# Graph attention in float32, one core: loads by graph in every step, a third buffer for transposed blocks, the reciprocal moved, the first graph reordered

## What is computed

```python
q, k, v = proj(Wq, bq), proj(Wk, bk), proj(Wv, bv)          # [32, 8, 256, 32]
scores = einsum('bhqd,bhkd->bhqk', q, k) * 32 ** -0.5
scores = scores * (adj + adj)[:, None]                      # a mask with values, not of zeros alone
attn = softmax(scores, axis=-1)
ctx = einsum('bhqk,bhkd->bhqd', attn, v)                    # heads put side by side: [32, 256, 256]
out = layernorm(x + einsum('bse,fe->bsf', ctx, Wo) + bo)    # [32, 256, 256]
```

## Time and profile before

| | |
|---|---|
| device time, 3 runs | median 437.6 us (437.01 to 439.08) |
| the profiled execution | 432.45 us, its span 430.8 us |
| PE busy | 383.4 us, 89% of the span |
| DVE busy | 387.9 us, 90% |
| ACT busy | 360.5 us, 84% |
| POOL busy | 249.6 us, 58% |
| DMA | mean 214 GB/s; 248 `carried<-boxes` of 192.0 KB, 124 `v_boxed<-v` of 64.0 KB, 16 masks and 16 x of 512.0 KB, 15 `xt` of 512.0 KB |

### The profile page before, as it was taken

How to read it: one execution, slowest core, us unless ns; L and a number is a source line. 1 busy time by engine, 2 the same in 40 slices (tenths; PEclk the granted TensorE clock), 3 DMA queues, 4 the chain that set the end, 5 groups by cost and what they waited for, 6 DMA issues and landing times.

```text
span 430.8 us, 12136 instructions
## 1 busy us (share of the span) xinstructions
PE 383.4 (89%) x3628; PEld 291.0 (68%) x3628; DVE 387.9 (90%) x1592; ACT 360.5 (84%) x1223; POOL 249.6 (58%) x379
## 2 busy tenths in 40 slices
PE   8968999998989899998999999899898999997682
PEld 6755767776767676675777667677766767775452
DVE  4687999999999999999899999989999999999965
ACT  4588899888888888888988888899888789988760
POOL 3330656748385664748567474856747385554455
PEclk9999999999999999999999999999999999999998
DMA  8548869788887978878797888889788787978632
GB/s 288 168 107 217 235 165 304 175 265 217 232 242 181 303 159 252 247 202 263 192 295 182 243 242 210 254 203 294 178 251 228 163 256 178 276 170 214 155 90 73
DMA packets 58658, 92.28 MB, mean 214 GB/s; under 512 B 7777, under 2 KB 47970, under 8 KB 58594
## 3 DMA queue, kind: packets, MB, share of 16 engines
q1 hardware_dynamic: 45266, 66.35, 60.8%
q10 hardware_dynamic: 13328, 25.17, 16.9%
HBM read 26.22 MB, written 8.39 MB: 80 GB/s over the span
## 4 chain that ended last, share of the span: by engine, by line
ACT 31%; PE 20%; DVE 16%; SPq 12%; issue 11%; DMA 7%; POOL 1%; ACTq 0%; DVEq 0%; POOLq 0%
ACT probs L705 24%; SPq L202 8%; DVE probs L502 8%; PE ctx_bank L396 5%; DMA v_boxed<-v 5%; DVE boxes L520 5%; PE proj_bank L325 4%; PE out_bank L343 4%; SPq L211 4%; PE row_bank L256 3%; ACT turned_probs L713 3%; ACT inverse L719 2%; PE turn_bank L273 1%; ACT kq L733 1%; DVE top L502 1%
## 5 line engine op out<-in xcount | busy, mean ns | idle before, releaser
L705 ACT ACTIVATE probs<-probs,low_top 128x256 f32<-128x256 f32 x512 | 254.7, 504 | 41.5 <-DVE low_top L511 40.4
L502 DVE CUSTOM_DVE_ANT_0 probs<-row_bank,adj_rows 128x256 f32<-128x256 f32 x512 | 188.0, 416 | 5.1 <-PE row_bank L256 4.8
L520 DVE STREAM_TRANSPOSE boxes<-probs 128x1536 f32<-128x1536 f32 x62 | 109.7, 1769 | 1.0 <-DMA carried<-boxes 1.0
L705 ACT ACTIVATION_READ_ACCUMULATOR probs<-probs,low_top 128x1 f32 x512 | 99.3, 194 | 0.0
L325 PE MATMUL proj_bank<-xt_parts,w_parts 128*128 128x512 f32 x360 | 99.3, 411 | 0.0
L325 PEld LDWEIGHTS proj_bank<-xt_parts,w_parts 128*128 128x128 f32 x360 | 63.0, 188 | 30.2 <-issue 19.6
L256 PE MATMUL row_bank<-kq 32*128 32x256 f32 x1024 | 73.3, 400 | 5.2 <-DVE top L502 3.9
L396 PE MATMUL ctx_bank<-carried,v_boxed 128*32 128x256 f32 x744 | 59.5, 382 | 19.1 <-DMA v_boxed<-v 16.1
L842 POOL COPY wide<-shares 128x512 f32<-128x512 f32 x32 | 19.5, 610 | 74.9 <-DVE shares L528 74.9
L396 PEld LDWEIGHTS ctx_bank<-carried,v_boxed 128*32 128x32 f32 x744 | 31.2, 109 | 43.5 <-issue 30.7
L413 PE MATMUL out_bank<-w_parts,ctx_parts 128*128 128x256 f32 x372 | 51.5, 287 | 9.9 <-issue 6.7
(11 more groups left out here) (85 smaller groups left out, 467.2 us busy)
## 6 DMA issues: line engine op xcount, KB each, us to landing
carried<-boxes SPq DMA_DIRECT2D x248, 192.0 KB, 4.0
adj_rows<-in_adj ACTq DMA_DIRECT2D x16, 512.0 KB, 6.6
xr<-in_x ACTq DMA_DIRECT2D x16, 512.0 KB, 6.9
v_boxed<-v SPq DMA_DIRECT2D x124, 64.0 KB, 2.5
out<-result ACTq DMA_DIRECT2D x31, 256.0 KB, 4.8
xt<-in_x_t SPq DMA_DIRECT2D x15, 512.0 KB, 4.2
xt<-in_x_t SPq DMA_DIRECT2D x2, 256.0 KB, 3.2
w_whole<-in_wk ACTq DMA_DIRECT2D x2, 128.0 KB, 3.4
```

The lines of the kernel that those rows point to most:

```text
L502: last = nc.vector.tensor_tensor_reduce(probs[:, h % RING, t * S:(t + 1) * S], row_bank[j][:, t * S:(t + 1) * S], adj_rows[:, (g // 2) % 2 ...
L520: nc.vector.transpose(boxes[:, n % 2].rearrange("p a h (f q) -> p (h f) a q", q=D), probs[:, first:first + BOXED, :].rearrange("p h (f a k ...
L705: last = nc.scalar.activation(tile, tile, ACT.Exp, bias=low_top[:, g % 2, J * c + j, t:t + 1], accum_out=sums[:, g % 2, t, j * T + c:j * T ...
```

## The change

- `xt`, masks and x are loaded by graph (for `xt`: by half of the feature rows) instead of by pair: 256 KB in every step. Masks of graph g + 2 are issued behind ACT's third head, x of graph g behind its seventh, one `xt` half in every step of SP. Each half has a semaphore.
- `boxes` has three buffers instead of two.
- `divide(g - 1)` goes from the end of DVE's step g - 1 into step g, behind the second head's row maxima.
- The first graph has an order of its own on PE, DVE and ACT: the second pair's keys are projected ahead of the first values, `rows(1)` follows at once, and the bias is made in step 1.

The diff, without the lines around it:

```diff
+BOXES = 3
...
-        boxes = sb("boxes", [P, 2, J, BOXED, P])
+        boxes = sb("boxes", [P, BOXES, J, BOXED, P])
...
-        xt_in, x_in, adj_in, stored, carried_in, v_in = (
-            [sem(f"{name}{n}") for n in range(2)] for name in ("xt_in", "x_in", "adj_in", "stored", "carried_in", "v_in"))
+        stored, v_in = ([sem(f"{name}{n}") for n in range(2)] for name in ("stored", "v_in"))
+        x_in, adj_in, carried_in = ([sem(f"{name}{n}") for n in range(4)] for name in ("x_in", "adj_in", "carried_in"))
+        xt_in = [[sem(f"xt_in{n}_{t}") for t in range(T)] for n in range(2)]
...
-            def load_x_t(pair):
+            def load_x_t(pair, t):
...
-                    sp.wait_ge(first_low, T)
-                wait(sp, xt_low, T * (pair - 2))
-                sp.dma_start(xt[:, pair % 2].rearrange("p t s -> p (t s)"), x_t[pair]).then_inc(xt_in[pair % 2], 16)
+                    sp.wait_ge(first_low, t + 1)
+                if pair > 2:
+                    sp.wait_ge(xt_low, T * (pair - 3) + t + 1)
+                sp.dma_start(xt[:, pair % 2, t, :], x_t[pair][:, t * 2 * S:(t + 1) * 2 * S]).then_inc(xt_in[pair % 2][t], 16)
...
-                                 boxes[D * i:D * (i + 1), n % 2].rearrange("p j h f -> p j (h f)")
-                                 ).then_inc(carried_in[n % 2], 16)
+                                 boxes[D * i:D * (i + 1), n % BOXES].rearrange("p j h f -> p j (h f)")
+                                 ).then_inc(carried_in[n % 4], 16)
...
-            load_x_t(1)
+            for t in range(T):
+                load_x_t(1, t)
...
-            load_x_t(2)
-            load_x_t(3)
+            for pair in (2, 3):
+                for t in range(T):
+                    load_x_t(pair, t)
...
-                if g % 2 == 1 and is_pair(g // 2 + 4):
-                    load_x_t(g // 2 + 4)
+                if g > 0 and is_pair((g + 1) // 2 + 3):
+                    load_x_t((g + 1) // 2 + 3, (g + 1) % 2)
...
-                    for c in range(T):
-                        pe.wait_ge(carried_in[c], 64 * (g + 1))
+                    for n in range(T * g, T * g + T):
+                        pe.wait_ge(carried_in[n % 4], 64 * (n // 4 + 1))
...
+            for half_ in range(2):
+                project_kq(1, 0, half_)
...
-            make_bias()
+            rows(1)
+            for half_ in range(2):
+                project_kq(1, 1, half_)
+            project_v(1)
+            turn_probs(0)
...
+                if g == 0:
+                    return
...
-                if 0 < g < B:
+                if g < B:
...
+                if g == 1:
+                    make_bias()
...
-                if h % (4 * J) == 0 and h % (2 * H) == 0:
-                    dve.wait_ge(adj_in[(g // 2) % 2], (g // 4) * 16 + 16)
+                if h % H == 0:
+                    dve.wait_ge(adj_in[g % 4], (g // 4) * 16 + 16)
...
-                wait(dve, carried_in[n % 2], 64 * (n // 2))
+                if n >= BOXES:
+                    dve.wait_ge(carried_in[(n - BOXES) % 4], 64 * ((n - BOXES) // 4 + 1))
...
-                nc.vector.transpose(boxes[:, n % 2].rearrange("p a h (f q) -> p (h f) a q", q=D),
+                nc.vector.transpose(boxes[:, n % BOXES].rearrange("p a h (f q) -> p (h f) a q", q=D),
...
+            read_first_q(0)
...
-            for c in range(T):
-                read_first_q(c)
+            read_first_q(1)
...
+                    if j == 1 and n % T == 0 and n > 0:
+                        divide(n // T - 1)
...
+                if g == 1:
...
-                if 0 <= g < LAST:
-                    divide(g)
...
-            def load_masks(pair):
+            def load_masks(g):
...
-                wait(act, rows_used, 16 * (pair - 1))
-                act.dma_start(flat(adj_rows[:, pair % 2]), adj[pair]).then_inc(adj_in[pair % 2], 16)
-            def load_x(pair):
-                wait(act, y_ready, 2 * (pair - 1))
-                act.dma_start(flat(xr[:, pair % 2]), x[pair]).then_inc(x_in[pair % 2], 16)
+                wait(act, rows_used, H * (g - 3))
+                act.dma_start(adj_rows[:, (g // 2) % 2, g % 2].rearrange("p t s -> p (t s)"),
+                              adj[g // 2][:, (g % 2) * T * S:(g % 2 + 1) * T * S]).then_inc(adj_in[g % 4], 16)
+            def load_x(g):
+                wait(act, y_ready, g - 3)
+                act.dma_start(xr[:, (g // 2) % 2, g % 2].rearrange("p t e -> p (t e)"),
+                              x[g // 2][:, (g % 2) * T * E:(g % 2 + 1) * T * E]).then_inc(x_in[g % 4], 16)
...
+            load_masks(1)
...
-                        copy_v(0)
...
-                    if s == 1 and g % 2 == 0 and is_pair(ahead):
-                        load_masks(ahead)
+                    if s == 1 and g == 0:
+                        copy_v(0)
+                    if s == 2 and is_graph(g + 2):
+                        load_masks(g + 2)
...
-                    if s == 2 and g % 2 == 0 and is_graph(g):
-                        load_x(g // 2)
-                    if s == 3 and is_graph(g + 1):
+                    if s == 6 and is_graph(g):
+                        load_x(g)
+                    if s == (3 if g > 0 else 5) and is_graph(g + 1):
...
-                    if s == 3 and is_pair(ahead):
+                    if s == (3 if g > 0 else 4) and is_pair(ahead):
...
+                pool.wait_ge(xt_in[pair % 2][t], 16 * loads(pair))
...
-                    pool.wait_ge(xt_in[pair % 2], 16 * loads(pair))
...
-                if b == 0:
-                    if pair == 0:
-                        pool.wait_ge(bias_ready, 1)
-                    pool.wait_ge(x_in[pair % 2], (pair // 2) * 16 + 16)
+                if pair == 0 and b == 0:
+                    pool.wait_ge(bias_ready, 1)
+                pool.wait_ge(x_in[2 * (pair % 2) + b], (pair // 2) * 16 + 16)
```

2 lines of the change are left out of this document (1 added, 1 removed).

## The result

The changed kernel takes **417.25 us** (median of 6 runs, 414.61 to 418.86) against 436.89 us before (median of 6 runs, 435.11 to 439.08): a ratio of 0.9547 with a 95% interval of 0.9506 to 0.9589, 4.5% less time. Its profiled execution is one of these runs, with 418.86 us and a span of 416.3 us. Throughout, a median is of all runs of a kernel, while a ratio leaves out those over 1.5% above the kernel's fastest.

What follows compares the result with a forecast made beforehand. Bound by the ring of reciprocals and first maxima and by late blocks at weigh_v in alternate steps; 432.45 - 16.9 (27 steps) - 5.5 (first graph) = 410.05 profiled, with the 5.15 us distance 415.0 us, range 409.5 to 424.

Steps and rivals of the forecast that it cites:

- The ring of the reciprocals: Once per graph DVE's reciprocals wait for ACT's last exponential (20.1 us), ACT's next first exponential for DVE's maxima (40.4 us).
- T = (17.33 + d) / 2: Lower limit on step T from the loop through PE's weigh_v; d is transpose end to last block landing.
- the 11.92 forecast: Mean step in us forecast for 27 steps, instead of 12.547, a gain of 16.9 us.
- DVE's floor, 11.82: A dense DVE step without its 0.41 us wait: 11.82 us, below which no step was to go.
- d = 6.5: Forecast us from transpose end to last block landing with loads by graph, no longer alternating between 6.0 and 7.3.
- the bound of 7.3: Upper bound in us for the new transpose-to-landing time, seen in one late delivery; the lower was 6.0.
- The first graph, 5.5 us: New order at the start: graph 3 to start at 47.2 us instead of 52.68, a gain of 5.5 us.
- The end, nothing: Step 30 is already 11.76 us and nothing behind it is changed, so no gain at the end.
- Three buffers, at most 1 us: Third block buffer removes DVE's wait before box, 1.0 us in all; at most 1 us, contained in the 11.92.
- 5.15 us between profiled execution and median: Median of three runs before lay 5.15 us above the profiled execution (437.6 against 432.45); same distance assumed after.
- 410.05 forecast for the profiled execution: Sum of the gains: 432.45 - 16.9 - 5.5 = 410.05 us, span 408.4.
- The rival by the constant part of a transfer: Slower, 3%: constant part occupies the queues, 2.2 us for each of 47 added transfers, step 13.7, about 463 us.

Runs made afterwards that it cites:

- the kernel that does not depend on them: Changed kernel with weigh_v(g - 2) behind project_v(g + 1) on PE and scale_context(g - 2) behind box(2g - 1) on DVE: 426.4 us, ratio 0.971.

## Why the prediction was right, and where it was not

The median of 417.25 us lies 2.25 above the 415.0 forecast and inside the range. The steps, in the order in which the prediction made them:

- **The ring of the reciprocals**: right. The wait went from 20.1 to 1.9 us; undoing the move alone costs 3.1 points. That it opens the way to steps shorter than 12.20 was shown by the kernel with the move undone, whose shortest common step is 12.22.
- **T = (17.33 + d) / 2**: the form right, the constant 0.2 too large. The loop runs over two steps, so its own test is their sum: from 205.32 us, where VectorE begins graph 16, to 229.25 it is 23.93 us, with a d of 6.79 for the blocks of graph 15, which PE needs in the second of these steps: d + 17.14. In 12 of the 14 places where PE waited over 0.3 us for blocks at the full clock the sum is d + 17.14 to within 0.02, and the same constant is the common one in the kernels with loads by pair. With the median d of 6.63 T is then 11.89. Without the two bad steps the mean is (327.39 - 16.19 - 13.49) / 25 = 11.91, against the 11.92 forecast. The steps do not settle at T but go 11.65, 12.0 and more, because a late `weigh_v` is made up for in the next step.
- **DVE's floor, 11.82**: 11.65 measured, though 11.76 stood in the earlier trace rows. The stretch of the earlier trace rows has no gap but the 0.41 us that I took off. About 0.08 of the 0.17 goes with that wait: in a dense step the operation behind `add_residual` starts 0.61 us after it, ahead of its end, and in the stretch its whole 0.69 us passed first. The rest is hundredths, over some fifty operations.
- **d = 6.5**: 6.6 in the common step. Left out were single landings of 9.1 and 8.5 us; the bound of 7.3 was that of one row, and the kernel before had no longer one than 8.0 in its profile. The steps behind them took 16.19 us (fourth stretch above) and, by ScalarE's timeline, 13.49, so they cost (16.19 - 11.92) + (13.49 - 11.92) = 5.8 us, of which 1.6 is the lower clock in the first (last section).
- **The first graph, 5.5 us**: graph 3 starts 52.68 - 48.16 = 4.5 us earlier, and I gave the gain to the wrong edit. The order has 1.4 us of it (1.9, counted from the first exponential); the reciprocals alone bring 2.2 (2.7). The rows at the start:

```profile
11.12 1.15 PE L264 MATMUL row_bank<-kq 32*128 32x256 f32 x16
...
17.03 0.42 DVE L521 CUSTOM_DVE_ANT_0 probs<-row_bank,adj_rows 128x256 f32<-128x256 f32 x1 [0.56 <-PE row_bank L264]
...
14.28 0.51 ACT L728 ACTIVATE probs<-probs,low_top 128x256 f32<-128x256 f32 x1 [3.18 <-DVE low_top L530]
...
25.31 0.52 ACT L728 ACTIVATE probs<-probs,low_top 128x256 f32<-128x256 f32 x1
...
36.23 0.53 ACT L728 ACTIVATE probs<-probs,low_top 128x256 f32<-128x256 f32 x1
...
48.16 0.51 ACT L728 ACTIVATE probs<-probs,low_top 128x256 f32<-128x256 f32 x1 [0.18 <-DVE low_top L530]
```

The second group came nearly as expected (17.03 instead of 19.68, 16.5 forecast), and graphs 0, 1 take 11.03 and 10.92 us on ACT. But the 0.52 us before the first scores bought little (PE starts them at 11.12 instead of 11.29, its projections ending later), the first exponential is at 14.28, not 13.65, and graph 2 took 11.93 us, not 11.1.
- **The end, nothing**: wrong by 1.5 us. At the start of PE's step 31 it waited 2.78 us for blocks, the clock was halved from 386.7 to 390.1, and graph 31 to the end took 29.1 instead of 27.6. With masks and x by pair, where the clock did not fall there, it took 27.8.
- **Three buffers, at most 1 us**: right in the changed kernel (0 to be seen), but not in general: 2 points with loads by pair.
- **5.15 us between profiled execution and median**: wrong. The changed kernel's profiled execution is 1.6 us above its median. In the terms of the sum the error was larger than the result shows: 410.05 forecast for the profiled execution, 418.86 measured, 8.8 us, of which 5.8 for the two late landings, 1.0 for the start, 1.5 for the end, 0.9 outside the span (418.86 - 416.3 against 432.45 - 430.8), and a few tenths back from the common steps. Of it 6.8 fell away again: before, the profiled execution was a fast example (432.45 against 436.89), after, it was a slow one (418.86 against 417.25), and 0.7 lies between the medians of three and of six runs before. So that the median came out within 2.25 us of the forecast is in good part luck. That landings which differ from run to run made the distance is argued, by the 0.84 us spread of the kernel that does not depend on them, and not shown.
- **The rival by the constant part of a transfer** (the Trainium skill, "DMA: Bandwidth & Descriptors", section "Anatomy of one DMA — SWDGE (gpsimd) path": some 2.0 us per DMA, for those that GpSimd issues; ours are SP's and ACT's): 47 transfers more, about 40 of them in the 27 steps, the same bytes, and the DMA share of the 27 steps is 0.88, where 0.83 x 12.547 / 12.126 = 0.86 would follow from the shorter steps alone: 0.02 of 327 us is 6.5 us, 0.16 us for each added transfer, where 2.2 would have had to appear. By the page's reading of the fixed part as completion latency, which this supports, it does not add up on the engines. The rival is out.

## What to carry to other kernels

When a wait between two engines is taken away, ask which transfer is then needed earlier, and write the path through it as an equation for the step: here the moved reciprocals gave under 1% alone, and 3.1 points where smaller loads let the blocks land in time. Spread loads evenly over the steps when a short transfer with a due time shares the queues; it is the latest landing that is paid for, not the mean. And before an operation is moved later to give a transfer time, write down the whole ring that it then belongs to.

## What the runs showed of the hardware

A late landing can cost more than its wait when PE stands still for it. In the changed kernel PE waited 3.21 us for blocks; from 134.1 us on the granted clock was 0.50 for 3.4 us (fifth stretch above), which is 1.2 instead of 2.4 GHz, and the groups of matmuls ran long:

```profile
133.03 1.35 PE L404 MATMUL ctx_bank<-carried,v_boxed 128*32 128x256 f32 x18 [3.21 <-DMA carried<-boxes]
...
135.62 1.12 PE L281 MATMUL turn_bank<-ident,probs 128*128 128x128 f32 x4
...
136.38 2.18 PE L351 MATMUL out_bank<-w_parts,xt_parts 128*128 128x256 f32 x12
```

From the start of `weigh_v` to that of `turn_probs` it takes 2.59 us here (1.86 in the kernel before, 202.59 to 204.45), and `project_v` lasts 2.18 us as against 1.68 there. From the start of `weigh_v` to VectorE's next step it takes 13.01 us here, and 11.43 behind the late landing of graph 19 (a wait of 1.93 us), where the clock stayed at 1.00: the lower clock cost 1.6 us. The kernel with loads by pair shows the two cases at the same place:

```profile
146.42 2.14 PE L402 MATMUL ctx_bank<-carried,v_boxed 128*32 128x256 f32 x18 [2.27 <-DMA v_boxed<-v]
...
198.50 1.27 PE L402 MATMUL ctx_bank<-carried,v_boxed 128*32 128x256 f32 x18 [2.10 <-DMA v_boxed<-v]
```

Behind the wait of 2.27 us the mean granted clock of the step is 0.89 and the step takes 15.31 us; behind the one of 2.10 it is 1.00, and the step takes 13.82 (the third and fourth stretch of that kernel). The length of the wait does not decide it. With the first graph's order back the clock fell at 73.7 us behind a wait of 1.91 us (a step of 15.10 us); with two buffers it stayed at 1.00 behind one of 3.04 us (14.30 us):

```profile
73.49 0.94 PE L404 MATMUL ctx_bank<-carried,v_boxed 128*32 128x256 f32 x8 [1.91 <-DMA v_boxed<-v]
...
133.29 1.27 PE L404 MATMUL ctx_bank<-carried,v_boxed 128*32 128x256 f32 x18 [3.04 <-DMA carried<-boxes]
```

So two executions with the same late landing can differ by the 1.6 us of one fall. The kernel before, with its longest such wait at 2.1 us, kept the full clock to 428.5 of its 430.8 us.
